# One ring of four PSUM banks, sum parts added in SBUF, and value blocks of two key tiles in an attention stage

## What is computed

```python
xn = layernorm(x)                        # x: 4 x 2048 x 512, float32
qkv = xn @ qkv_w.T + qkv_b               # 16 heads of 32
attn = softmax(q @ k.T * 32 ** -0.5)     # per batch and head, 2048 x 2048
o = attn @ v
out = x + (o @ proj_w.T + proj_b) + moe(xn)   # moe: top 2 of 8 experts per batch element
```

## Time and profile before

| | |
|---|---|
| median of three runs | 5174.25 us (5173.32 to 5175.8) |
| the profiled execution | 5168.91 us, its span 5167.1 us |
| mean granted TensorE clock | 0.988 |
| attention stage within the span | about 1320 to 4972 us |

### The profile page before, as it was taken

The page is one execution under the profiler, slowest core; times in us unless marked ns, Lnnn a source line. Parts: engine busy times, 40 slices in busy tenths (PEclk is TensorE's granted clock), DMA queues, the critical chain, the costliest instruction groups (busy, mean ns, idle before and its releaser), DMA issues. The chain is left out here.

```text
span 5167.1 us, 83198 instructions
## 1 busy us (share of the span) xinstructions
PE 5031.4 (97%) x25932; PEld 2893.7 (56%) x25932; DVE 3420.5 (66%) x5616; ACT 2592.6 (50%) x4717; POOL 3231.8 (63%) x861
## 2 busy tenths in 40 slices
PE   8999999999899999999999999999999999999979
PEld 6878878788444444444444444444444444444447
DVE  4232232322678888877887887888788788888724
ACT  2121121211266666666666666666666666666631
POOL 1212111121488888887887888788788788888830
PEclk9999999999799999999999999999999999999989
DMA  5253343533402021121202102120220202020046
GB/s 171 88 158 95 117 130 97 153 94 106 102 20 53 17 52 42 32 53 24 50 19 56 48 22 53 24 50 20 57 50 20 56 18 50 20 56 17 7 164 238
DMA packets 186069, 348.49 MB, mean 67 GB/s; under 512 B 17956, under 2 KB 51748, under 8 KB 177448
## 3 DMA queue, kind: packets, MB, share of 16 engines
q1 hardware_dynamic: 185640, 342.99, 23.8%
HBM read 208.19 MB, written 134.22 MB: 66 GB/s over the span
## 5 line engine op out<-in xcount | busy, mean ns | idle before, releaser
L829 DVE TENSOR_REDUCE unit_max<-mx_ps 128x1 f32<-128x512 f32 x4096 | 2547.3, 682 | 664.0 <-PE mx_ps L890 617.8
L766 POOL TENSOR_TENSOR p_pair<-p_sb 128x2048 f32<-128x2048 f32 x512 | 2365.4, 4636 | 664.3 <-PE sum_ps L910 334.1
L814 ACT ACTIVATE p_sb<-st_ps 128x512 f32<-128x512 f32 x4096 | 2217.5, 599 | 1109.0 <-PE st_ps L951 1094.5
L890 PE MATMUL mx_ps<-k_x,q_x 96*128 96x512 f32 x4096 | 1734.9, 437 | 35.9 <-DMA k_x<-k_lo_d 19.6
L951 PE MATMUL st_ps<-q_x,k_x 97*128 97x512 f32 x4096 | 1621.1, 402 | 18.1 <-ACT p_sb L814 18.1
L890 PEld LDWEIGHTS mx_ps<-k_x,q_x 96*128 96x128 f32 x4096 | 771.6, 191 | 1042.5 <-DVE unit_max L829 787.6
L902 PE MATMUL o_ps<-p_sb,v_sb 128*32 128x512 f32 x8192 | 1093.8, 606 | 0.7 <-ACT p_sb L814 0.7
L951 PEld LDWEIGHTS st_ps<-q_x,k_x 97*128 97x128 f32 x4096 | 777.8, 190 | 239.2 <-ACT p_sb L814 120.1
L285 POOL TENSOR_TENSOR h_lo<-h_f,h_hi 128x512 fp32r<-128x512 f32 x128 | 165.0, 1290 | 689.1 <-DVE h_hi L469 689.1
L756 POOL TENSOR_TENSOR p_pair<-p_pair 128x2048 f32<-128x2048 f32 x128 | 587.5, 4590 | 10.0
L469 DVE CAST h_hi<-h_f 128x512 fp32r<-128x512 f32 x128 | 55.0, 431 | 540.7 <-ACT h_f L342 540.7
(11 more groups left out here) (92 smaller groups left out, 3708.4 us busy)
## 6 DMA issues: line engine op xcount, KB each, us to landing
q_x<-q_hi_d SPq DMA_DIRECT2D x128, 256.0 KB, 5.3
k_x<-k_hi_d SPq DMA_DIRECT2D x30, 1024.0 KB, 9.8
xt<-x SPq DMA_DIRECT2D x64, 256.0 KB, 2.7
stage<-w SPq DMA_DIRECT2D x32, 512.0 KB, 5.1
q_hi_d<-qk_hi SPq DMA_DIRECT2D x64, 256.0 KB, 3.0
q_lo_d<-qk_lo SPq DMA_DIRECT2D x64, 256.0 KB, 3.8
k_hi_d<-qk_hi SPq DMA_DIRECT2D x64, 256.0 KB, 2.6
k_lo_d<-qk_lo SPq DMA_DIRECT2D x64, 256.0 KB, 3.3
```

Source lines behind the costliest of these rows:

```text
L766: pool.tensor_tensor(p_pair[:, slot, :, :], p_sb[:, 2 * i % SLOTS, :, :], p_sb[:, (2 * i + 1) % SLOTS, :, :], ALU.add).then_inc(pair_done, 1)
L814: act.activation(p_sb[:, kt % SLOTS, h, :], st_ps[bank(g, m)][:, :], ACT.Exp, scale=SCALE).then_inc(exp_done, 1)
L829: dve.reduce_max(unit_max[:, n // 4, n % 4:n % 4 + 1], mx_ps[n % 3][:, :], AX.X).then_inc(unit_done, 1)
L890: pe.matmul(mx_ps[n % 3][:, :], q_x[qc][0:R, h, t * P:(t + 1) * P], k_x[u][0:R, h, kc * 512:(kc + 1) * 512], start=True, stop=True).then_i ...
```

## The change

- PSUM: `sum_ps` is gone and `mx_ps` has four banks, one ring (RING) that units, the turned maxima and the sum parts fill in the order of STEPS (FILLS, PLACE). Each fill waits for the reading of the fill four before (`emptied`), counted by one semaphore `bank_read`.
- Sum parts: those taken at one place are accumulated in their ring bank, and VectorE copies the first place's bank to `sum_raw` and adds the others to it (`gather`), five passes of 128 x 512 in a group.
- Value products: STEPS has one V in a pair, which makes the products of the two key tiles of the pair before.
- Inverses: `sum_raw` holds each head's sums 32 times. A transfer spreads one copy over 128 partitions (`spread_sums`, 128 x 16), VectorE inverts that (`invert`), and SyncE stores it in HBM, waits, and loads it back to 32 partitions per head (`spread_inverse`).
- The product of output and inverse is made by GpSimd before its last addition (NORM = 9) and not by VectorE.
- Loads of the next quad: keys of two heads at qc = 0, one head at qc = 1 and 2, values at qc = 3.

```diff
-        STEPS = ["USUSUSVZUSUSUSUSVUS", "USUSUSVZUSUSUSUSVUS", "USUSUSVUSUSUSUSVUS", "USUSUSVUSUSUSUSVUS",
-                 "USUSUSVZUUSUSUSUSVUS", "USUSUSVUUSUSUSUSVUS", "SSSVZTSUSUSUSUVSUU", "USUSUSVZUSUSUSUSVUS"]
+        STEPS = ["SUSSUVZUSUSUSUSUSU", "SUSSUVZUSUSUSUSUSU", "SUSSUVUSUSUSUSUSU", "SUSSUVUSUSUSUSUSU",
+                 "SUSSUVZUSUSUSUSUSU", "SUSSUVUSUSUSUSUSU", "SUSSUVZTUSUSUSUSUSU", "SUSSUVZUSUSUSUSUSU"]
...
-        mx_ps = [ctx.enter_context(nc.psum_tensor(f"mx_ps{i}", [P, 512], F32)) for i in range(3)]
+        mx_ps = [ctx.enter_context(nc.psum_tensor(f"mx_ps{i}", [P, 512], F32)) for i in range(RING)]
-        sum_ps = ctx.enter_context(nc.psum_tensor("sum_ps", [P, TOK], F32))
...
+                def spread_sums(read):
+                    sp.wait_ge(bank_read, read)
+                    sp.dma_start(sum_t[:, :], sum_raw[0:P:D, :]).then_inc(sum_ld, 16)
+                def spread_inverse(count):
+                    sp.wait_ge(inv_done, count)
+                    sp.dma_start(inv_d.rearrange("h (r n) -> (h r) n", n=QR), inv_t[:, :]).then_inc(inv_st, 16)
+                    sp.wait_ge(inv_st, count * 16)
+                    if not (isinstance(count, int) and count == 1):
+                        sp.wait_ge(o_st, (count - 1) * 16)
+                    for h in range(4):
+                        sp.dma_start(o_inv[h * D:(h + 1) * D, :], inv_d[h, :].partition_broadcast(D)).then_inc(inv_ld, 16)
...
-                            load_keys(it + 1 if isinstance(it, int) else it + 1, 1 - u)
-                            load_values(it + 1, 1 - u)
+                            load_keys(it + 1, 1 - u, slice(0, 2))
                         if qc > 0 and more:
                             sp.wait_ge(st_ready, L * G * SK + g * SK)
+                            if qc < 3:
+                                load_keys(it + 1, 1 - u, slice(qc + 1, qc + 2))
+                            else:
+                                load_values(it + 1, 1 - u)
                             load_queries(it + 1, qc - 1)
...
+                        if not (first and g == 0):
+                            spread_sums(read_count(L, g, PART_PLACE[LAST_PART], first, last))
                         if not (last and g == G - 1):
                             load_shift(L * G + g + 2, (qc + 1) % QC)
                         if not (first and g == 0):
+                            spread_inverse(L * G + g)
                             store_group(L, it - 1 if qc == 0 else it, (qc - 1) % QC, L * G + g)
...
+                def normalise(count):
+                    pool.wait_ge(inv_ld, count * 64)
+                    pool.wait_ge(o_copied, count)
+                    pool.tensor_tensor(o_inv[:, :], o_raw[:, :], o_inv[:, :], ALU.mult).then_inc(o_done, 1)
...
+                            if n == NORM and not (first and g == 0):
+                                normalise(L * G + g)
...
-                    act.activation(sum_raw[:, :], sum_ps[:, :], ACT.Copy).then_inc(sum_copied, 1)
...
-                    dve.reciprocal(o_inv[:, cols], sum_raw[:, cols]).then_inc(inv_done, 1)
...
+                def gather(groups, at, place, read):
+                    dve.wait_ge(sum_done, groups * NS + PARTS_BY[at])
+                    if at == PARTS_AT[0]:
+                        if not (isinstance(groups, int) and groups == 0):
+                            dve.wait_ge(sum_ld, groups * 16)
+                        dve.tensor_copy(sum_raw[:, :], mx_ps[place % RING][:, :]).then_inc(bank_read, 1)
+                    else:
+                        dve.wait_ge(bank_read, read)
+                        dve.tensor_tensor(sum_raw[:, :], mx_ps[place % RING][:, :], sum_raw[:, :], ALU.add).then_inc(bank_read, 1)
+                def invert(count):
+                    dve.wait_ge(sum_ld, count * 16)
+                    if not (isinstance(count, int) and count == 1):
+                        dve.wait_ge(inv_st, (count - 1) * 16)
+                    dve.reciprocal(inv_t[:, :], sum_t[:, :]).then_inc(inv_done, 1)
...
+                def emptied(L, g, place, first, last):
+                    if place - RING == TURNED:
+                        pe.wait_ge(shift_done, L * G + g + 2)
+                    elif not (first and reads(g, place - RING, first, last) == 0):
+                        pe.wait_ge(bank_read, read_count(L, g, place - RING, first, last))
...
-                    if n >= 3:
-                        pe.wait_ge(unit_done, base + n - 2)
-                    pe.matmul(mx_ps[n % 3][:, :], q_x[qc][0:R, h, t * P:(t + 1) * P], k_x[u][0:R, h, kc * 512:(kc + 1) * 512],
+                    pe.matmul(mx_ps[UNIT_PLACE[n] % RING][:, :], q_x[qc][0:R, h, t * P:(t + 1) * P], k_x[u][0:R, h, kc * 512:(kc + 1) * 512],
...
-                        op = pe.matmul(sum_ps[h * D:(h + 1) * D, :], ones[:, :], p_pair[:, slot, h, :], start=(i == 0), stop=(i == NS - 1))
+                        op = pe.matmul(mx_ps[place % RING][h * D:(h + 1) * D, :], ones[:, :], p_pair[:, slot, h, :],
+                                       start=(i == PARTS_BY[at] - PARTS_ON[at]), stop=(i + 1 == PARTS_BY[at]))
...
-                            values(L, g * KT + kt, u, kt)
+                            for kt in (2 * j - 2, 2 * j - 1):
+                                values(L, g * KT + kt, u, kt)
```

More of the change, by code:

```diff
@@ new lines, in attention_stage, with filled @@
+        PLACE = {(j, i): p for p, (j, i, _) in enumerate(FILLS)}
+        PLACES = -(-len(FILLS) // RING) * RING
+        TURNED = [p for p, (_, _, step) in enumerate(FILLS) if step == "T"][0]
+        UNIT_PLACE = [p for p, (j, _, step) in enumerate(FILLS) if step == "U" and j >= AHEAD]
+        UNIT_PLACE += [p for p, (j, _, step) in enumerate(FILLS) if step == "U" and j < AHEAD]
+        def filled(step, j, g, first, last):
+            if step == "U":
+                return not (last and g + (2 if j >= AHEAD else 1) >= G) and (g > -2 or j >= AHEAD)
+            return step == "Z" and not (first and (g < 0 or g == 0 and j < 2))
@@ new lines, in reads @@
+        def reads(g, place, first, last):
+            if place < 0:
+                return reads(g - 1, place + PLACES, first, last)
+            if g < 0 and not first:
+                return -sum(step != "T" for _, _, step in FILLS[place + 1:])
+            return sum(filled(step, j, n, first, last) for n in range(-2 if first else 0, g + 1)
+                       for p, (j, _, step) in enumerate(FILLS) if n < g or p <= place)
+        READS = sum(step != "T" for _, _, step in FILLS)
+        FIRST_READS = reads(G - 1, PLACES, True, False)
@@ new lines, in read_count @@
+        def read_count(L, g, place, first, last):
+            n = reads(g, place, first, last)
+            return n if first else (L * G + g + 1) * READS + (n + FIRST_READS - (G + g + 1) * READS)
+        PARTS_AT = sorted({at for _, _, at in PARTS})
+        PARTS_IN = sum(at < NP for at in PARTS_AT)
+        LAST_PART = PARTS_AT[-1]
+        PART_PLACE = {at: PLACE[at % NP, STEPS[at % NP].index("Z")] for at in PARTS_AT}
+        PARTS_ON = {at: sum(at == x for _, _, x in PARTS) for at in PARTS_AT}
@@ L649, in unit_at, with part_before @@
+        PARTS_BY = {at: sum(x <= at for _, _, x in PARTS) for at in PARTS_AT}
+        ALL_READS = read_count(TURNS - 1, G - 1, PLACES, False, True)
+        def part_before(at):
+            if at == PARTS_AT[0]:
+                return 0
+            old = PARTS_AT[PARTS_AT.index(at) - 1]
+            return PART_PLACE[old] - (PLACES if at >= NP > old else 0)
         def unit_at(j, i):
@@ L664, in bank_read @@
             return [n for n in range(-SB, 0) if bank(G, n) == bank(0, m)][0] + 1
-        assert units_of(AHEAD - 1)[-1] == UN - 1 and "".join(STEPS).count("U") == UN
+        assert units_of(AHEAD - 1)[-1] == UN - 1 and "".join(STEPS).count("U") == UN and TURNED >= RING
         assert all(step.count("S") == 8 for step in STEPS)
@@ L779, in turn_shift @@
                         act.wait_ge(shift_ld, (count - 1) * 16)
[L780 removed]
+                    act.activation(shift[:, :], mx_ps[TURNED % RING][0:4 * TT, 0:P], ACT.Copy, scale=-1.0).then_inc(shift_done, 1)
                 def copy_o(count):
@@ L803, in turn @@
                                     copy_o(L * G + g)
-                                if m == 8 + 3 and not (first and g == 0):
-                                    copy_sum(L * G + g)
                                 if m == 8 * AHEAD + 3 and not (last and g == G - 1):
@@ L982, in turn @@
                                 elif step == "V":
-                                    products(2 * j - 1 + STEPS[j][:i].count("V"))
+                                    products(j)
                                 elif step == "Z":
-                                    sum_parts(j)
+                                    sum_parts(j, PLACE[j, i])
                                 elif not (last and g == G - 1):
@@ L992, in _ @@
                 turn(TURNS - 1, False, True)
```

(6 more changed lines are left out.)

148 lines of the change are left out of this document (79 added, 69 removed).

## The result

The changed kernel takes 5083.18 us (median of four runs, 5080.82 to 5083.65), the kernel before 5173.78 beside it (four runs, 5166.76 to 5175.80). The ratio is 0.9827, 95% interval 0.9812 to 0.9842. The forecast was 5060 with a range of 4985 to 5145: faster, as expected, but by 91 us and not by 114. The profiled execution took 5082.81 us, its span 5081.0. I compare its trace with that of before.

The account below looks back on a forecast made before the run. TensorE, busy 97%, was taken to bound the kernel. A group falls from 55.72 to 53.8 us, saving 121 over 63 groups, minus 7 for the tail: 114, so 5055 profiled, 5060 as median; range 4985 to 5145.

Parts of the forecast that it names:

- Blocks of two key tiles: TensorE's value products: eight fewer switches per group save 2.5 us; waiting on ScalarE gives back 0.24 of each 0.31.
- Rival (a): Merged stretch of matmuls: ScalarE doesn't bind, stretch 5.81 us, total about 4935; chance 0.13, including results between it and forecast.
- Fourth bank: PSUM ring: no unit waits for VectorE's reductions, so 1.4 us of old waits per group go.
- no wait of U on VectorE: Expected sign in the new TensorE trace: no unit matmul stands waiting for a VectorE reduction.
- rival (b): Old waits return elsewhere, such as a bank handed on late around sum parts: 1 to 1.5 us per group, about 5143; chance 0.14.
- near misses: Sixth and seventh scores of a stretch may slip waiting for the third and fourth exponentials: 0.1 us per group allowed.
- the old waits of 1.4: TensorE's waits for VectorE or ScalarE in the old order, 1.4 us per group, taken as gone.
- Sum parts added by VectorE: Five more VectorE passes per group at 0.69 us each, taken to cost nothing; TensorE's sum parts unchanged.
- Rival (c): VectorE's addition fights GpSimd for SBUF: 2.19 us instead of 0.69, total about 5313; chance 0.06.
- Inverse by transfers: Inverse through HBM stays hidden: there at about 50.5 us, before GpSimd's 53.2; decides only when two landings pass 11 us.
- Rival (d): Inverse comes late: beyond 11 us of landings each further us costs one per group, 13 to end slower; chance 0.03.
- The tail: Last group and final steps: GpSimd's chain +1.3 us, longer addition, transfer and inverse sequence +6.1, together +7.4, once.

Follow-up runs that it names:

- the run with the score first: Changed kernel with a score as first matmul after the value products, strict turns of units and scores, ScalarE's copies one exponential earlier: 4990.41 us, ratio 0.9654.
- the ring of 70: Changed kernel with ring places counted as the 70 fills a group really has, not padded to 72: 5024.93 us, ratio 0.9718.
- three deep: Each fill waits for the reading of the fill three before, not four, against the ring of 70: 5168.30 us, ratio 0.9995.

## Why the prediction was right, and where it was short

**Blocks of two key tiles.** Right in mechanism and, at one place, in size: V at 4.17 after the first U in the loop, forecast 4.18. The eighth score waits for the fifth exponential, and taking that wait away brings the stretch to 5.80, against 5.81 forecast. A stretch without Z took 6.02 in the loop, forecast 6.05. By the experiments the merge is worth 0.84 per steady group in the loop, where the sum gave 8 x 0.07 = 0.6. The rows of the forecast came from inside the loop. In the turns written out V comes at 4.04, so more than half of the wait of 0.24 is there only in the loop. Rival (a) is refuted, since the run with the score first is faster by 93 us.

**Fourth bank.** This is the step that failed. The walk gave every unit the bank of the fill four before and ended with "None waits". That holds inside a group only. Where two groups meet, the padding to 72 places leaves the ring two deep, and a unit waits 0.87 each time. The sign "no wait of U on VectorE" failed with it. In kind it is rival (b), a bank handed on late near Z, for 0.93 us per group instead of 1 to 1.5. The 0.1 that I put in for near misses was not needed: in the ring of 70 the period is 53.3, against the sum's 53.7 without it. That the old waits of 1.4 are gone was right. With the ring of 70 and one V per key tile the period is 54.11, where tiles without waits add up to 54.3. With merged blocks and three deep, 143 us come back, so the fourth bank is the larger part of the gain there.

**Sum parts added by VectorE.** Right. The groups by line, for the reduction, the addition and GpSimd's product:

```profile
L903 DVE TENSOR_REDUCE unit_max<-mx_ps 128x1 f32<-128x512 f32 x4096 | 2512.0, 681 | 217.7 <-PE mx_ps L978 210.3
...
L920 DVE TENSOR_TENSOR sum_raw<-mx_ps,sum_raw 128x512 f32<-128x512 f32 x256 | 177.1, 692 | 489.7 <-PE mx_ps L998 489.7
...
L828 POOL TENSOR_TENSOR o_inv<-o_raw,o_inv 128x512 f32<-128x512 f32 x64 | 82.4, 1288 | 9.7 <-DMA o_inv<-inv_d 9.7
```

The addition takes 691 to 693 ns in all 256, beside a GpSimd that is busy nearly all the time. Rival (c) is refuted. It is one PSUM and one SBUF input, where the product that took 4.72 had two from SBUF.

**Inverse by transfers.** Right: hidden. DMA issues, form, times, KB and median us to landing:

```profile
o_inv<-inv_d SPq DMA_DIRECT2D x256, 64.0 KB, 2.0
...
inv_d<-inv_t SPq DMA_DIRECT2D x64, 8.0 KB, 1.7
```

The two landings together are 3.7 us, where 11 would have decided. The product at 2516.94 stands directly between two additions, and pair 7 follows at 2518.47. Rival (d) is refuted. The stores of 64-byte pieces landed in 1.7 us, no later than the 8 KB loads of the shift (1.8). (In the Trainium skill, DMA: Bandwidth & Descriptors, the rule on pieces under 512 bytes stands in the table "Specifications". The section that the forecast names has a fixed cost per packet instead.) But it gained nothing either: with the reciprocals on VectorE the time is the same within 3 us.

**The tail.** Forecast +7.4, measured +6.1: from the copy of the output of the 63rd group to the next stage's first load of weights it is 63.5 before (4909.10 to 4972.63) and 69.6 after (4817.14 to 4886.74). The order of the steps is as forecast, answering to the earlier trace rows, and they take 8.9 us where 10.4 was forecast. The product is GpSimd's and takes 1.26, where the sum had VectorE's 0.7:

```profile
4874.98 0.69 DVE L920 TENSOR_TENSOR sum_raw<-mx_ps,sum_raw 128x512 f32<-128x512 f32 x1 [5.39 <-PE mx_ps L998]
4875.70 0.58 SPq L746 DMA_DIRECT2D sum_t<-sum_raw  x1
4877.57 0.25 DVE L927 RECIPROCAL inv_t<-sum_t 128x16 f32<-128x16 f32 x1 [1.89 <-DMA sum_t<-sum_raw]
4877.85 0.34 SPq L751 DMA_DIRECT2D inv_d<-inv_t  x1
4879.31 1.71 SPq L756 DMA_DIRECT2D o_inv<-inv_d  x4
4882.65 1.26 POOL L828 TENSOR_TENSOR o_inv<-o_raw,o_inv 128x512 f32<-128x512 f32 x1 [9.72 <-DMA o_inv<-inv_d]
```

**Not in the forecast: the loop.** I took one steady group of the hardware loop for all. Groups on constants are 0.96 shorter, and each of five jumps costs some 6 us in place of some 3.

**The sum again**, over the 62 periods from the first copy to the 63rd. Before 3470.95, after 3379.43, saved 91.5. Forecast 62 x 1.9 = 118. Less 62 x 0.93 = 57.7 where groups meet. Plus 62 x 0.5 = 31 for stretches shorter than the sum (53.3 against 53.8). Plus 14 x 0.96 = 13.4 for groups on constants. Less 14.3 for the jumps and the few odd groups: over steady periods alone the 62 hold 16.3 more before and 30.6 more after. This gives 90.4. So the forecast came this close partly by luck, because two errors ran against each other: the wait at the meeting was missed, and the rest was taken some 45 us too dear.

**What stays open.** Why a jump of the loop costs TensorE 3.4 us of "issue" now and 1.95 before. It comes with the merged blocks; a ring of 70 or of three deep, and the place of the inverse, don't change it (3.0 to 4.0 in those runs). With the score first there are two stops at each jump, of 3.1 to 3.7 and 2.1 to 2.7. What in the merged order does it is not shown. (The Trainium skill, Advanced Engine Details and Errata, "Control Flow Timing", gives about 108 ns for a compare-and-branch. The 3.4 us of the trace are thirty times that, so it is not the branch alone.) Which part of the 0.1 later hand-over in the loop is the register in the wait is open too: writing the loop out took both away together. How the 95 us besides the merge divide is open as well: three deep loses 143 with merged blocks, but it was not tried with blocks of one key tile.

## What to carry to other kernels

When a ring's places are rounded up to a multiple of its banks, the last and first fills of an iteration stand closer than the ring is deep: count the fills between each wait and its release across the seam, not only inside the body. When a change lets the bounding engine run closer behind another, an operation that was free before (here a product of two SBUF inputs beside a busy GpSimd) can cost more than the change gains. Read a jump of the hardware loop and a written-out iteration apart from a steady one before multiplying.

## What the hardware showed that I had not expected

- VectorE's product of two SBUF operands of 128 x 512 took 4.66 us on average where GpSimd's additions of 4.58 stood in a row: its length is mostly what is left of the running addition, plus 0.55, and 5.15 to 5.39 where it began at most 0.33 before the end of one and was held by the next as well. In the old order that was 2.19; in the tail, with GpSimd done, it was 0.69. The addition of PSUM and SBUF stayed at 0.69.
- After the stop of TensorE of 3.43 us shown above, the granted clock was 0.50 for some 6.5 us. In the kernel before, a stop of 1.95 was followed by as long a stretch at 0.50. After the change, the group was 6.3 to 6.6 us longer than its neighbours: 3.4 by the stop, 1.7 by the slower value block, the rest in the matmuls beside it.
- The same eight exponentials and their hand-overs took 4.14 us inside the loop, where the engines wait on a register's value, and 4.03 in the turns written out, on constants.
